# Four-stage image pipeline on one core: the first convolution three images ahead, and a prologue on three DMA queues

## The reference

```python
x = x + _L0_conv_ref(_gn(x), L0_conv_weights, L0_conv_biases)  # A: 3x3 convolution, zero padding, bias
x = x + _L1_conv_ref(_gn(x), 5)          # B: Newton-Schulz inverse of each 128 x 128 channel
x = x + _L2_conv_ref(_gn(x), L2_conv_weight)   # C: 3x3 convolution, circular padding
x = x + _L3_conv_ref(_gn(x), L3_conv_K)  # D: 3x3 convolution, zero padding, last row and column zero
# B, with W the normed image, per channel:
scale = norm1 * norminf                  # largest column sum and largest row sum of |W|
X = W^T / scale
for _ in range(5):
    X = X @ (2 I - W @ X)
```

## Time and profile before

| | us |
|---|---|
| median of 3 runs (lowest, highest) | 725.62 (724.13, 728.28) |
| the profiled execution, its own time | 727.48 |
| its span, first to last instruction | 725.7 |
| busy: PE, DVE, ACT, POOL | 607.9, 533.2, 383.5, 198.6 |
| mean granted TensorE clock | 0.954 of full speed |

### The profile page before, as it was taken

How to read it: one execution, slowest core, us unless ns; L and a number is a source line. 1 busy time by engine, 2 the same in 40 slices (tenths; PEclk the granted TensorE clock), 3 DMA queues, 4 the chain that set the end, 5 groups by cost and what they waited for, 6 DMA issues and landing times.

```text
span 725.7 us, 11297 instructions
## 1 busy us (share of the span) xinstructions
PE 607.9 (84%) x3752; PEld 507.1 (70%) x3752; DVE 533.2 (73%) x1304; ACT 383.5 (53%) x559; POOL 198.6 (27%) x289
## 2 busy tenths in 40 slices
PE   0695679749989989899899989999999969995956
PEld 0464667748777777778778778778777858884644
DVE  3855976666796878797797779887978687648551
ACT  0351437424666566664667456656677436753632
POOL 5122023112252224231242315222423122201302
PEclk9998999969999999999999999999999998998888
DMA  5186001950379322971488334942372135222352
GB/s 152 54 106 186 1 30 34 148 182 30 90 82 268 75 81 52 158 209 44 101 85 255 86 85 71 237 121 64 75 241 53 35 80 168 53 74 70 85 132 58
DMA packets 89124, 76.43 MB, mean 105 GB/s; under 512 B 6572, under 2 KB 81228, under 8 KB 86252
## 3 DMA queue, kind: packets, MB, share of 16 engines
q1 hardware_dynamic: 87548, 74.07, 44.6%
q0 software_dynamic: 1536, 1.86, 1.0%
HBM read 38.14 MB, written 24.25 MB: 86 GB/s over the span
## 4 chain that ended last, share of the span: by engine, by line
PE 38%; DVE 35%; ACT 8%; issue 7%; SPq 7%; DMA 4%; POOL 1%; DVEq 0%; ACTq 0%
PE conv_ps L750 23%; DVE zl L1005 6%; PE z L831 3%; DVE stB L676 3%; DVE bn_D L538 2%; DVE bn_A L538 2%; PE z L833 2%; PE z L835 2%; PE z L826 2%; ACT d_A L650 2%; PE z L840 2%; ACT zh L938 2%; DVE d_C L615 2%; DMA rows_dram<-x 1%; SPq L377 1%
## 5 line engine op out<-in xcount | busy, mean ns | idle before, releaser
L1005 DVE SCALAR_TENSOR_TENSOR zl<-z,zh 128x1024 fp32r<-128x1024 f32 x128 | 154.4, 1219 | 73.4 <-ACT zh L938 70.9
L938 ACT ACTIVATE zh<-z 128x1024 fp32r<-128x1024 f32 x128 | 130.2, 1019 | 69.6 <-PE z L835 36.8
L831 PE MATMUL z<-zh 128*128 128x256 f32 x512 | 154.3, 301 | 15.2 <-DVE zl L1005 15.2
L833 PE MATMUL z<-zl,zh 128*128 128x256 f32 x512 | 146.9, 287 | 0.0
L835 PE MATMUL z<-zh,zl 128*128 128x256 f32 x512 | 146.5, 286 | 0.0
L750 PE MATMUL conv_ps<-d_A,w_D 128*96 128x512 f32 (+1 forms) x432 | 104.5, 391 | 17.3 <-DVE w_D L608 16.5
L831 PEld LDWEIGHTS z<-zh 128*128 128x128 f32 x512 | 100.1, 196 | 24.1 <-DVE zl L1005 21.0
L750 PE MATMUL conv_ps<-d_C,w_C 128*96 128x512 f32 (+1 forms) x486 | 113.9, 382 | 0.7 <-issue 0.6
L750 PE MATMUL conv_ps<-d_A,w_A 128*96 128x512 f32 (+1 forms) x378 | 95.5, 401 | 14.7 <-DVE w_A L608 10.8
L833 PEld LDWEIGHTS z<-zl,zh 128*128 128x128 f32 x512 | 100.4, 196 | 1.0
L835 PEld LDWEIGHTS z<-zh,zl 128*128 128x128 f32 x512 | 100.1, 195 | 0.0
(11 more groups left out here) (182 smaller groups left out, 899.7 us busy)
## 6 DMA issues: line engine op xcount, KB each, us to landing
x<-x_dram SPq DMA_DIRECT2D x14, 1024.0 KB, 6.6
win_C<-rows_dram SPq DMA_DIRECT2D x40, 256.0 KB, 5.5
rows_dram<-x SPq DMA_DIRECT2D x32, 256.0 KB
win_A<-x SPq DMA_DIRECT2D x48, 160.0 KB
win_D<-out_C SPq DMA_DIRECT2D x7, 1056.0 KB, 6.8
y<-out_D SPq DMA_DIRECT2D x42, 168.0 KB, 3.9
x_dram<-out_A SPq DMA_DIRECT2D x30, 192.0 KB, 2.1
win_D<-out_C SPq DMA_DIRECT2D x14, 160.0 KB, 5.8
```

The lines of the kernel that those rows point to most:

```text
L831: pe.matmul(z[s][:, m, :], zh[s][:, m, 0:128], zh[s][:, m, :], start=False, stop=True, skip_group_check=True)
L833: pe.matmul(z[s][:, m, :], zh[s][:, m, 0:128], zl[s][:, m, :], start=False, stop=True, skip_group_check=True)
L938: act.activation(zh[s][:, :, :], z[s][:, :, :], ACT.Copy, scale=ROOT[j]).then_inc(s_zh[s], 1)
L1005: dve.scalar_tensor_tensor(zl[s][:, :, :], z[s][:, :, :], ROOT[j], zh[s][:, :, :].bitcast(f32), ALU.mult, ALU.subtract).then_inc(s_zl[s], 1)
```

## The change

A runs three images ahead of B in place of two. Image 2's A (`cA2`, in C's buffers, like image 0's, `cA0`) and two thirds of image 3's stand in cycle 0, the rest of image 3's in cycle 1, and from cycle 1 on A of image i + 3 stands in slots 17 to 23. The loop is cycles 2 and 3; cycle 4 has no load, and cycle 5 has no A. In cycles 5 to 7 C's groups stand in slots 9, 11, 13, 15, 17 and 19. In the prologue the windows of x and the rows of x1 are dealt out to SP, ACT and POOL by the window's number modulo 3, and each group of windows has its own semaphores. Image 2's first statistics are made there, and the absolute sums stand ahead of `dve_rows_B_var`, while `dve_rows_B_end` comes after the scales. The two small products of the norms go to `spare_ps`, and the chain of the norms has its own semaphore.

```diff
-        cA1 = Lodger("A1", cA, cC)
+        cA0, cA2 = Lodger("A0", cA, cC, cC, cC, cC), Lodger("A2", cA, cC, cC, cC, cC)
...
-        SP_X, POOL_X = (0, 1, 2, 5), (3, 4)
-        SP_ROWS, POOL_ROWS = (0, 2, 3, 5), (1, 4)
+        ON_SP, ON_ACT, ON_POOL = 0, 1, 2
...
+        def load_x(eng, b, queue):
+
+            win = A_of(b).win
+            eng.wait_ge(s_zero, b + 1)
+            for g in range(NG):
+                k0, kn = SPLIT_G[g]
+                for k in range(k0, k0 + kn):
+                    if k % 3 == queue:
+                        h0 = window_row(k)
+                        lo, hi = max(h0, 0), min(h0 + WIN, H)
+                        eng.dma_start(win[(lo - h0) * C:(hi - h0) * C, k, :],
+                                      x[bass.ds(b, 1), :, lo:hi, :].rearrange("b c h w -> (b h) c w"))\
+                            .then_inc((s_x01p if queue == ON_POOL else s_x01)[b][g], 16)
...
+            if is_int(i, 0):
+                for g in range(4):
+                    store_x1(sp, 2, g)
             store_x2(sp, i, 0)
             store_x2(sp, i, 1)
+            if is_int(i, 0):
+                store_x1(sp, 2, 4)
+                store_x1(sp, 2, 5)
...
             if has_A:
-                store_x1(sp, i + 2, 0)
-                store_x1(sp, i + 2, 1)
-                store_x1(sp, i + 2, 2)
+                store_x1(sp, i + 3, 0)
+                store_x1(sp, i + 3, 1)
+            if has_A and not is_int(i, 0):
+                store_x1(sp, i + 3, 2)
             if load:
-                load_x_rows(sp, i + 3)
+                load_x_rows(sp, i + 4)
...
+        D_SLOTS, C_SLOTS, A_SLOTS = (1, 2, 3, 5, 6, 7), (9, 10, 11, 13, 14, 15), (17, 18, 19, 21, 22, 23)
+        FILL = {
+            "start": {**groups_at("A2", 4, 6, 8, 10, 12, 14), **groups_at("A", 17, 19, 21, 23)},
+            "second": {**groups_at("A3", 2, 5, first=4), **groups_at("C", *C_SLOTS), **groups_at("A", *A_SLOTS)},
+            "full": {**groups_at("D", *D_SLOTS), **groups_at("C", *C_SLOTS), **groups_at("A", *A_SLOTS)},
+            "late": {**groups_at("D", *D_SLOTS), **groups_at("C", 9, 11, 13, 15, 17, 19)},
+            "last": {**groups_at("D", *D_SLOTS), **groups_at("C", 9, 11, 13, 15, 17, 19)},
+        }
...
+                if is_int(i, 0) and q == 2:
+                    win_sqrt(act, cA2, 2)
+                if is_int(i, 0) and q in (1, 2, 3, 5, 7, 9):
+                    high_parts(act, cA2, 2, (1, 2, 3, 5, 7, 9).index(q))
...
+                if is_int(i, 0) and q == 1:
+                    win_stats_3(dve, cA2, 2)
+                if is_int(i, 0) and q == 2:
+                    win_stats_4(dve, cA2, 2)
+                    win_weights(dve, cA2, 2)
...
-            with eng.Fori(2, B - 3) as i:
+            with eng.Fori(2, B - 4) as i:
                 cycle(eng, i, True, True, True, True, True)
-            cycle(eng, B - 3, True, True, True, True, False)
+            cycle(eng, B - 4, True, True, True, True, False)
+            cycle(eng, B - 3, True, True, False, True, False)
...
-            for g in SP_X:
-                load_x(sp, 1, g)
-            for g in SP_ROWS:
-                rows_from_windows(sp, 0, g)
+            load_x(sp, 1, ON_SP)
             load_x_rows(sp, 2)
+            for g in range(NG):
+                rows_from_windows(sp, g, ON_SP)
+            load_x_rows(sp, 3)
...
+            load_x(act, 0, ON_ACT)
+            load_x(act, 1, ON_ACT)
+            win_sqrt(act, cA0, 0)
...
+            for g in range(NG):
+                conv_out(act, cA0, 0, g)
+                rows_from_windows(act, g, ON_ACT)
...
+            win_stats_1(dve, cA2, 2, 0, 1, 2)
...
             link_B = dve_rows_B_mean(dve, 0)
-            dve_rows_B_var(dve, link_B, 0)
-            dve_rows_B_end(dve, link_B, 0)
             for ch in range(NCHK):
                 dve_abs(dve, 0, ch, bank[ch])
+            dve_rows_B_var(dve, link_B, 0)
             dve_norm_top(dve, 0)
             dve_norm_scale(dve, 0)
+            win_stats_2(dve, cA2, 2)
+            dve_rows_B_end(dve, link_B, 0)
             cycles(dve, dve_cycle)
...
-            row_var_B(pe, 0)
             for ch in range(NCHK):
                 pe_norm_T(pe, 0, ch, bank[ch])
+            row_var_B(pe, 0)
             pe_norm_sums(pe, 0)
             pe_norm_spread(pe, 0)
```

380 lines of the change are left out of this document (199 added, 181 removed).

## The result

| | before | changed |
|---|---|---|
| median of 4 runs each, same chip (lowest, highest) | 726.95 (724.13, 732.15) | 738.73 (737.58, 741.75) |
| ratio, 95% interval | | 1.0165 (1.0119 to 1.0211) |
| the profiled execution, its own time | 727.48 | 739.71 |
| its span | 725.7 | 737.9 |
| busy: PE, DVE, ACT, POOL | 607.9, 533.2, 383.5, 198.6 | 612.5, 539.1, 383.5, 197.9 |

What follows compares the result with a forecast made beforehand. Bounds taken by stage: prologue a load and statistics chain, three-convolution cycles over 92% PE-busy. Terms -7.8 + 4.0 - 4.4 - 0.7 - 6.1 - 1.8 + 1.0 = -15.8 from the 725.6 median gave 710 us, range 698 to 718.

Steps and rivals of the forecast that it cites:

- x's first image on three queues: Prologue: image 0's windows land at about 11.0 us, so DVE ends the first statistics 6.2 us earlier.
- rival 2: First loads: the DMA engines, not the issue, bound them, so the first term falls to 0; 716 us, chance 0.14.
- x1's rows on three queues, image 2's statistics in between: Prologue: last row landed at 40 us, DVE's row statistics start at 41.9, a gain of 5.4 us in all.
- Absolute sums ahead of the variance: Prologue: DVE's sums start some 3 us earlier, -2.4 us; ends 0 and -3.
- Without that cover 4.1: Prologue: Newton steps and image 2's second statistics cost nothing in DVE's 5.09 us idle time, 4.1 us without it.
- Cycle 0: Cycle 0: four added convolution groups and 2.4 us more DVE work cost +4 us in the first half, 0 in the second.
- Cycle 1: Cycle 1, first half: C's windows load ends about 4.4 us earlier and the new groups hide in the wait; -4.4 us.
- Cycles 5 to 7: Late cycles: no A in cycle 5 and C's groups in later slots; -6.1, -1.8 and +1.0 us.
- rival 3: Cycles 0 and 1: moved groups aren't hidden, cycle 0 pays all 8.4 us, SP comes no earlier; 719 us, chance 0.07.
- the slower case in the late cycles: Late cycles: the wait on the copy into D's windows is longer, delaying x2 and the next cycle; 731 us, chance 0.05.
- no wait on win_D: Cycles 5 and 6, slot 21: prediction wrong if DVE's DMA wait for D's windows is absent or over 5 us.
- cycle 0 over 74 us: Cycle 0: expected about 70 us long; prediction wrong if it is over 74 us.

Runs made afterwards that it cites:

- e3: Changed kernel with image 1's windows issued only after all windows of image 0 have landed; 740.4 us.
- e9: Kernel before with the prologue's part alone (three queues, semaphores for each group, sums ahead of the variance), A two images ahead; 720.95 us, ratio 0.9918.
- e2: Changed kernel with x1's rows issued ahead of the loads of images 2 and 3, image 2's first statistics after the row mean; 735.03 us.
- e14: e13 with SP issuing no load of image 2 or 3 until all of x1's rows have landed; 726.12 us, ratio 0.9964 to the kernel before.
- e13: e12 without e1's wait, x1's rows issued ahead of both images' loads, image 2's first statistics behind the scales; 725.32 us, ratio 0.9966 to the kernel before.
- e1: Changed kernel with SP waiting until all of x1's rows have landed before it issues image 3's loads; 735.85 us.
- e12: Changed kernel, A three images ahead, with e1's wait, e3's order and e10's place for the bases; 731.14 us, ratio 1.0036 to the kernel before.
- e6: Changed kernel with the bases of C's and D's weights built in the prologue behind image 2's statistics, not in cycle 0; 732.52 us.
- e5: Changed kernel with each of image 2's A groups in cycle 0 making one of its nine matmuls; 739.27 us.
- e10: e9 with e3's order, and the bases of C's and D's weights built before the first statistics; 718.48 us, ratio 0.9878 to the kernel before.
- e8: Kernel before with C's groups of cycles 6 and 7 moved to slots 9, 11, 13, 15, 17, 19; 731.35 us, before 731.31.
- e11: e10 with C's groups of cycles 6 and 7 in slots 9, 11, 13, 15, 17, 19; 717.99 us, ratio 0.9891 to the kernel before.
- e4: Changed kernel with C's groups of cycles 5 to 7 back in slots 9, 10, 11, 13, 14, 15; 744.8 us.

## Why the prediction was wrong, step by step

Two terms failed. The rows of x1 and DVE's start on them, forecast as a gain of 5.4 us, were a loss of 9.5, because the last copy's landing was taken from a trace without loads in front, and ACT's own copies and image 2's statistics were priced at too little. And cycle 0, forecast at +4, cost 13.4, because DVE's work in its first half was put at 2.4 us more and was 10.6 more.

**x's first image on three queues (-6.2; it was -2.3).** The mechanism held and the size was off. The statistics' end (L568) came at 16.83 for 19.14 at L521. Eight windows left SP in 5.99 us, about as worked out, but the windows landed later than the 11.0 that the sum assumed: in the chain

```profile
7.30 7.93 DMA win_C<-x
```

is a landing of 7.93 us where I took 4.2 from the earlier trace rows. Image 1's windows were issued right behind on all three queues; e3 takes them away and gets 2.4 us back. This is rival 2's mechanism, for 2.4 of the 3.9 us that were missing; the other 1.5 stay open. In e9 the same loads gained 4.0 us (the same step at 15.10). By the Trainium skill ("DMA: Bandwidth & Descriptors", Issuing engines are not separate DMA queues) nothing but sequencer time is saved; the runs lie between the rule taken strictly and my term. The sequencer time saved was 3.4 us of SP's 9.41. ACT's price, which I had bounded by nothing below, was 5.69/7 = 0.81 us for each issue, near SP's:

```profile
1.19 5.69 ACTq L330 DMA_DIRECT2D win_C<-x  x7
```

**x1's rows on three queues, image 2's statistics in between: the step that failed.** "At 35 us the last, landed at 40" was wrong twice. The last copy can't be issued before ACT has put out the last group, at 41.1; SP came to it only at 43.79, since its row copies took 0.76 to 3.36 us each to issue, where they took 0.73 to 0.85 in the kernel before and in e2. And I took a landing of 5 us from a trace in which no bulk loads stood in front of the copies. The kernels of the study fill the table (last issue to landing, or to DVE's start where it waited for the rows):

| | no loads right behind | loads right behind |
|---|---|---|
| no loads in front | e14: 45.94 - 42.64 = 3.3 | e2: 44.70 - 40.64 = 4.1; e9 3.7, e13 4.0, before 5.0 |
| image 2's loads in front | e1: 7.58; e12 7.5 | changed: 12.92; e3 13.8 |

In these runs loads behind cost 5.3 us only when loads in front have left a backlog. The cause is the order on SP: image 2's loads stand in front of the copies because its statistics were to be made early.

Even with the rows there in time this step would have gained nothing. I had DVE at image 2's statistics at 37.5 and through at 41.9; it was there at 44.75 and through at 49.1, later than the kernel before begins its row statistics (47.26). The 2.3 us that DVE was ahead with the first statistics were gone when it ended image 1's low parts (43.72; before 43.70). In between the chain passes through ACT's row copies, priced at nothing: the two before the last group's output stand in it with 0.73 and 0.76 us, one earlier with 0.73. In e9 too a lead of 4.0 us had shrunk to 0.8 there (42.88). That ACT's copies ate the lead is read from the chain; no run takes them away. So of the 14.9 us between forecast (41.9) and run (56.74) about half, 7.2, is DVE late, and 7.6 its wait for the rows. Start of the row statistics: +9.5 us (56.74 for 47.26) where I had forecast -5.4 for both prologue steps on it. In e9, without image 2, it is 44.05 (-3.2).

**Absolute sums ahead of the variance (-2.4).** Right in e9, smaller in the changed kernel. From the start of the row statistics to the maximum 13.0 us for 14.4 in the changed kernel (-1.4; DVE waits 1.15 and 2.27 us in front of the first two), and 12.1 in e9 (-2.3). What I costed at nothing, the Newton steps and image 2's second statistics behind the scales, was not hidden: four steps that I took at 0.2 to 0.3 us each lasted about 1 us, and DVE came to its first zl at 78.40 with PE idle:

```profile
71.77 1.08 DVE L605 TENSOR_SCALAR col_A<-mv_A,col_A 128x2 f32<-128x2 f32 x1
72.89 0.95 DVE L606 TENSOR_TENSOR col_A<-col_A 128x2 f32<-128x2 f32 x1
73.88 0.96 DVE L607 TENSOR_TENSOR col_A<-col_A,mv_A 128x2 f32<-128x2 f32 x1
74.87 0.96 DVE L567 TENSOR_TENSOR col_A<-col_A,cst 128x1 f32<-128x1 f32 x1
...
78.40 2.35 DVE L1076 SCALAR_TENSOR_TENSOR zl<-z,zh 128x1024 fp32r<-128x1024 f32 x2
```

```profile
79.68 0.39 PE L906 MATMUL z<-zh 128*128 128x256 f32 x1 [2.06 <-DVE zl L1076]
```

"Without that cover 4.1" was in the prediction; the cover was there (5.09 us) and too short.

**Cycle 0 (+4; it was +13.4, +11.0 of it in the first half).** I counted PE's groups and gave DVE 2.4 us more. It got 10.6: 33.96 us for 23.36. About 5.9 of these are not new work but steps that took longer beside a POOL instruction: four column steps of image 2's (L606, L607, L567, L533) 0.95 to 1.05 for 0.16 each, the rounding of its weights (L654) 1.30 for 0.31, four sums of the bases (L1174) 0.86 for 0.46 in the mean. The stage was at 0.81 of its length busy on DVE, in a chain of round trips. It followed DVE's work (e6: 6.1 us less, and 4.4 to 6.2 shorter) more than PE's (e5: 6.9 less, and 1.4 to 3.2 shorter). The six bases stood in that stage before the change already (4.4 us), and cost there too: e10's first half is 28.4 us for e9's 32.6. So the stage wasn't free on DVE, as the prediction had it with its 7.7 us, when image 2's steps were added.

PE's term was too small as well: busy for 33.5 us where I had 22.0 + 8.4 = 30.4, alone more than the 31.1 us that the stage had lasted. The prediction doesn't name the rival that this points to, the granted TensorE clock. It was 0.84 in this stage for 0.88; in the 10 us from 50 to 60, where the changed kernel waits for the rows and PE is busy for 0.5 us, it fell to 0.63; the first row is the changed kernel's, the second the one before:

```profile
50.00:60.00 10.00, 0.50 (x3) 0.50 (x3) 2.71 (x8) 0.00 (x0) 0.00 (x0) 0.63 0.81 108
50.00:60.00 10.00, 5.82 (x38) 4.67 (x38) 6.31 (x19) 1.48 (x4) 4.03 (x4) 1.00 1.13 171
```

How long a stretch can become at a lower clock with its instructions unchanged, e8 shows: those of the kernel before, 3.2 us longer at 0.80 for 0.88. No run holds the clock and changes the work, so how much of the 11 us is the clock's stays open.

In the second half, costed at 0, it was +2.4 (37.8 for 35.5); e13 has the same 37.6, e11 34.2. Here too the clock was lower where it was longer (0.95 for e11's 1.00), and PE busy for 31.8 us for 30.4. This part stays open: e5 brought it to 35.8, so here the matmuls count.

**Cycle 1 (-4.4; it was -3.0).** The mechanism held, the size was smaller. SP issued the store of x2's last edge 4.6 us into the cycle in place of 7.2. ACT waits less for C's windows, which come 19.4 us into the cycle in place of 22.8. The first half's 39.5 us are the shortest of all executions with these instructions; e1 to e4, e6 and e12 to e14 have 40.2 to 41.3, for 42.4 before, so the gain is rather 1 to 2 us:

```profile
172.18 0.72 ACT L694 ACTIVATE d_C<-win_C,col_C 128x512 fp32r<-128x512 f32 x1 [4.22 <-DMA win_C<-rows_dram]
```

**Cycles 5 to 7 (-6.9 in all; it was -5.4).** The gain came mostly from A's absence (e4). The first halves did not lose the 2.1 us of C's group: cycle 5's is 39.2 us for the 37.4 forecast, and cycle 6's 39.4 to 41.0 for 39.5 before. PE stands 2.25 us at 505.18 for DVE's sums, which speaks for DVE's pace; no run tests it. In cycle 7, without norms, it was -2.1. The second halves are 32.4 for 33.1, and the wait on the copy that I had expected at slot 21 is not there: SP issues it from 602.85, 20.9 us after slot 12 as I had worked out, but DVE comes to the first window (L615) only at 612.37, without a wait. Only in cycle 7 does the copy end the chain, with D's weights 1.3 us later.

**The rivals.** None of the five was it, though two had a part: rival 2 in the first term, and rival 3 in cycle 0, where more than its 8.4 us were paid, but not for PE's groups. I looked for the slower case in the late cycles, with 0.05, and the copy there costs nothing up to cycle 6 and 1.3 us in cycle 7. Two of the prediction's own signs of being wrong came true: no wait on win_D, and cycle 0 over 74 us. What decided was a load put in front of a small copy that the chain needs, in a prologue where the DMA share is 0.68 already in the kernel before (0.82 in the changed one), and work given to DVE in a stage that followed DVE's work the most.

## What to carry to other kernels

Running further ahead moves work, it doesn't remove it: cost the stage that receives it by the engines in its own chain, and not by the engine that has the most work over the whole. Before you put bulk loads on a queue ahead of small copies that the first result waits for, add their backlog to the landing of the copies, since a landing time read from a trace without them doesn't hold. And a change of several parts should be tried in parts: here the prologue's part alone is 0.8% faster (0.9918), the whole 1.65% slower.
